# Taking a row maximum ahead of the PSUM ring reads of its tick, and holding back GpSimd's bias copies, in a software-pipelined attention kernel

## What is computed

```python
x = x + _L0_conv_ref(_gn(x), Wq, Wk, Wv, Wo, rel_pos_bias, particle_rel_pos_bias)   # softmax attention, 8 heads, additive bias
t = _to_tokens(x)
t = t + _L1_attn_ref(_ln_t(t), Wq, Wk, Wv, W1, b1, w2, b2)                          # additive attention
t = t + _L1_ffn_ref(_ln_t(t), gate_w, w1, b1, w2, b2)                               # 8 experts, top 2
```

```python
A = jnp.einsum('bse,he->bsh', q, W1[:, :e]) + b1
B = jnp.einsum('bse,he->bsh', k, W1[:, e:])
hidden = jnp.tanh(A[:, :, None, :] + B[:, None, :, :])
logits = jnp.einsum('bijh,h->bij', hidden, w2) + b2[0]
attn = jax.nn.softmax(logits, axis=-1)
return jnp.einsum('bij,bjd->bid', attn, v)
```

## Time and profile before

| | |
|---|---|
| median of 3 executions | 2275.16 us |
| the three | 2275.16, 2265.41, 2275.72 us |
| the profiled execution: its time | 2264.8 us |
| its span, first to last instruction | 2263.0 us |
| mean granted TensorE clock | 0.979 |
| busy share PE, ACT, DVE, POOL | 91%, 74%, 69%, 68% |
| L1510, L1512 and L952 | 96 of each |

### The profile page before, as it was taken

One profiled execution on the slowest core, in us unless ns is written; L12 is line 12 of the kernel. 1 busy time (PEld: TensorE's weight loads), 2 busy tenths in 40 slices (PEclk: granted clock), 3 DMA queues, 4 the chain that ended last, 5 costly groups with the idle time before them and its releaser, 6 DMA issues.

```text
span 2263.0 us, 54452 instructions
## 1 busy us (share of the span) xinstructions
PE 2056.6 (91%) x19545; PEld 1203.6 (53%) x19545; DVE 1550.5 (69%) x4167; ACT 1682.2 (74%) x1966; POOL 1535.5 (68%) x1907
## 2 busy tenths in 40 slices
PE   4889999999999999999999999999999978799996
PEld 2555555555555555455555555555545443367775
DVE  7786777777777787878787878787867554324343
ACT  4449888888887878888888888888879998524332
POOL 5117667677676767676767676767677876347777
PEclk8799999999999999999999999999999999999998
DMA  4746322222322232223223232323221000035553
GB/s 108 111 86 145 93 46 69 48 63 47 72 50 72 51 71 51 71 52 69 53 63 59 61 60 60 58 59 54 58 44 26 13 5 6 24 57 87 85 88 34
DMA packets 157429, 137.41 MB, mean 61 GB/s; under 512 B 24666, under 2 KB 149815, under 8 KB 157105
## 3 DMA queue, kind: packets, MB, share of 16 engines
q1 hardware_dynamic: 119376, 109.87, 23.8%
q0 software_dynamic: 23824, 16.85, 5.4%
q10 hardware_dynamic: 13968, 7.30, 1.3%
HBM read 82.68 MB, written 54.52 MB: 61 GB/s over the span
## 4 chain that ended last, share of the span: by engine, by line
PE 29%; DVE 18%; issue 16%; POOL 14%; POOLq 10%; DVEq 5%; ACT 5%; DMA 1%; another core or an unknown queue 0%; SPq 0%; ACTq 0%
POOL hidden L847 10%; PE logits L1052 8%; POOLq L846 7%; POOL out_dram L601 4%; DVE max_halves L1324 3%; PE av_bank L1038 3%; PE ring L1130 3%; PE ring L1144 2%; ACT hidden L969 2%; PE scores L1022 2%; PE scores L1025 2%; ACT hidden L976 2%; PE ring L1152 2%; PE ring L1121 1%; DVE logit_bias L1510 1%
## 5 line engine op out<-in xcount | busy, mean ns | idle before, releaser
L847 POOL TENSOR_SCALAR hidden<-b_rep,a_cols 128x768 f32<-128x768 f32 x1120 | 1026.8, 921 | 415.3 <-issue 232.2
L969 ACT ACTIVATE hidden<-hidden 128x2304 f32<-128x2304 f32 (+1 forms) x384 | 796.1, 2073 | 52.9 <-POOL hidden L847 52.8
L1052 PE MATMUL logits<-hidden,w_shifted 128*32 128x384 f32 x6144 | 580.6, 494 | 58.2 <-ACT hidden L976 31.1
L1324 DVE TENSOR_REDUCE max_halves<-ring 128x4 f32<-128x512 f32 (+1 forms) x704 | 451.0, 659 | 156.8 <-PE ring L1130 150.9
L945 ACT ACTIVATE probs<-scores 128x512 f32<-128x512 f32 (+1 forms) x768 | 391.5, 547 | 202.5 <-PE scores L1025 195.9
L976 ACT ACTIVATE hidden<-b_rep,a_cols 128x768 f32<-128x768 f32 x416 | 385.0, 933 | 0.0
L1052 PEld LDWEIGHTS logits<-hidden,w_shifted 128*32 128x32 f32 x6144 | 163.4, 109 | 290.8 <-issue 227.4
L1130 PE MATMUL ring<-k_max,q_max 112*128 112x128 bf16 x2688 | 270.3, 223 | 17.2 <-DVE max_halves L1324 12.8
L1022 PE MATMUL scores<-bias_q,onehot_k 112*128 112x512 bf16 (+1 forms) x768 | 273.9, 357 | 4.1 <-DMA q_parts<-max_parts 1.8
L1025 PE MATMUL scores<-q_parts,k_parts 98*128 98x256 bf16 (+1 forms) x1536 | 275.0, 260 | 0.0
L1130 PEld LDWEIGHTS ring<-k_max,q_max 112*128 112x128 bf16 x2688 | 180.9, 99 | 157.9 <-issue 66.3
(11 more groups left out here) (274 smaller groups left out, 2611.7 us busy)
## 6 DMA issues: line engine op xcount, KB each, us to landing
qk_parts<-qk_parts_sb SPq DMA_DIRECT2D x16, 1152.0 KB, 4.3
q_parts<-qk_parts SPq DMA_DIRECT2D x192, 96.0 KB, 3.2
k_parts<-qk_parts SPq DMA_DIRECT2D x192, 96.0 KB, 4.4
q_max<-qk_parts SPq DMA_DIRECT2D x96, 96.0 KB
k_max<-qk_parts SPq DMA_DIRECT2D x96, 96.0 KB
expert_rows<-clear_row ACTq DMA_DIRECT2D x9, 792.0 KB, 5.2
x_in<-in_x_dram SPq DMA_DIRECT2D x96, 64.0 KB
x<-in_x_dram SPq DMA_DIRECT2D x96, 64.0 KB
```

The lines of the kernel that those rows point to most:

```text
L847: last = g.tensor_scalar(hidden[:, q % SLOTS, o, :], b_rep[:, side], 1.0, a_cols[:, side, a_col(q, o):a_col(q, o) + 1], ALU.mult, ALU.add)
L969: s.activation(hidden[:, t % SLOTS, 0:n_, :], hidden[:, t % SLOTS, 0:n_, :], ACT.Tanh)
L1052: last = mm(logits[32 * g:32 * g + 32, half, 0:HALF], w2_shifted[:, k, :], hidden[:, q % SLOTS, g, HALF * half:HALF * half + HALF], start= ...
L1324: v.tensor_reduce(max_halves[:, h % 4:h % 4 + n_, BLOCK_PAIRS.index((qb, kb))], bank[:, 0:n_ * P].rearrange("p (h k) -> p h k", h=n_), AX. ...
```

## The change

DVE's block of maximum and bias moves from the end of slot 1, after the reads, to slot 0, ahead of the reads of its tick. GpSimd waits for `parts_ready` to reach 4 before its first bias copy. No instruction is added or taken out besides that wait.

```diff
@@ GpSimd, prepare()
                 g.memset(flag[:, 0:1], 0.0).then_inc(bias_made, 1)
+                pool.wait_ge(parts_ready, 4)
                 for h in range(H):
                     last = g.tensor_copy(bias_q[0:64, h, :].rearrange("p (b n t) -> p b n t", n=16, t=8),
@@ VectorE, body(ps)
                     for slot in range(PARTS):
-                        for use in parts[slot]:
-                            if ps.has(use[0]):
-                                read(ps, use)
-                        if t % 4 == 0 and slot == 1 and ps.has(stage) and blk >= 0:
+                        if t % 4 == 0 and slot == 0 and ps.has(stage) and blk >= 0:
                             c = ps.batch(stage)
                             dve.wait_ge(logits_added, c * 24 + 4 * (blk + 1))
                             if positive(count := c * 6 + blk):
@@
                             dve.drain()
                             v.tensor_scalar(logit_bias[:, 1:2], logit_bias[:, 0:1], b2_col[:], b2_col[:], ALU.subtract,
                                             ALU.add).then_inc(max1_ready, 1)
+                        for use in parts[slot]:
+                            if ps.has(use[0]):
+                                read(ps, use)
```

## The result

The changed kernel is slower: its median is 2291.53 us (2287.85 to 2296.0, five executions) where the kernel before has 2269.34 (2261.03 to 2275.72) in the same series. The ratio is 1.0103, its 95% interval 1.0076 to 1.0129: 1.0% slower, 22 us. The forecast was no change, 2270 us, and its range ended at 2283. The profiled execution's span is 2293.5 us (before 2263.0), the mean granted clock 0.973 (before 0.979).

A forecast was written before the change was run, and what follows sets the result against it. No single engine was taken to set the pace; the chain changes hands between PE, DVE and GpSimd. Terms -1.8 - 1.1 = -2.9 us, from the two levels' mean 2270.3, gave 2267.4, leaned to 2270 us; range 2253 to 2283.

The forecast's parts named there:

- Ticks 4 and 0: Earlier maximum gives PE 0.91 us at tick 4 and at most 0.38 at tick 0, up to 1.29 us by tick 7.
- not under 35: Sign to look for: ScalarE's waits ahead of its exponential L952 fall from 70.8 to under 35 us.
- the first rival: GpSimd doesn't decide: every full pass keeps its 1.29 us, 17.9 us or 0.8% faster; chance 0.15.
- Tick 7: "nothing ahead of them has moved": In nine passes GpSimd's sums decide when the tanh ends; nothing ahead of those sums moved, so the gain is zero.
- The term of 0.9 us in four passes: At tick 7, passes 1, 5, 6 and 7 have about 1 us of slack and keep 0.9 us each.
- Tick 8: 0.45 us lost, net 1.8 us: Later read of ring use 8.0 costs PE 0.45 us in four passes, leaving 4 x (0.9 - 0.45) = 1.8 us gained.
- Tick 12: Read of 12.1 comes 1.33 us later, within 1.66 us of slack: no effect.
- the rival that VectorE starves: Late ring reads at tick 12 leave DVE an empty ring: +14.4 us, 0.6% slower; chance 0.11.
- Tick 16: "Nothing is queued behind it that PE needs sooner": Cast L1408 goes behind the maximum; DVE is 0.56 us late, at most 1.47, under 1.64 us of idle time: no cost.
- my own price if the cover were gone: At tick 16, without idle time to absorb DVE's lateness, the cost would be 13 x 0.56 = 7.3 us.
- Tick 20: Only the order of DVE's maximum and the two cuts of the transpose changes: no effect.
- GpSimd's copies: In the head, held-back bias copies shorten DVE's second long subtraction from 1684 to 558 ns, 1.13 us gained.

The follow-up runs named there:

- max_0_4_fetch_32: Kernel before with the maximum ahead at ticks 0 and 4, the bias wait and eight dummy matmuls (32 instructions) in PE's head: 2272.89 us, ratio 1.0016.
- after_fetch_32: The whole changed kernel with 32 more instructions in front of PE's program: 2283.29 us, ratio 1.0059 to the kernel before.
- max_8_12_20: Kernel before with the maximum ahead at ticks 8, 12 and 20 only, no bias wait: 2267.52 us, ratio 0.9988.
- max_8_to_20_hold: Kernel before with the maximum ahead at ticks 8, 12, 16 and 20, the bias wait, and GpSimd's tick 21 sums held: 2261.98 us, ratio 0.9968.
- the hold: GpSimd's sums of tick 21 wait until DVE has made the first three normalized heads; added to the whole changed kernel: 2274.13 us, ratio 1.0026 to before.
- max_not_16: Changed kernel with tick 16 alone undone (maximum ahead at ticks 0, 4, 8, 12, 20, with the bias wait): 2280.93 us, ratio 1.0063 to before.
- bias_alone: Kernel before with only GpSimd's wait ahead of its bias copies, every maximum in its old place: 2267.88 us, ratio 0.9993.
- max_16: Kernel before with the maximum ahead at tick 16 alone, no bias wait: 2281.92 us, ratio 1.0064.
- max_16_hold: Kernel before with the maximum ahead at tick 16 alone, and GpSimd's sums of tick 21 held until three heads are made: 2260.49 us, ratio 0.9971.
- fetch_48: Kernel before with twelve dummy matmuls (48 instructions) in PE's head: 2298.38 us, ratio 1.0129.
- fetch_32: Kernel before with eight dummy matmuls (32 instructions) in PE's head: 2267.42 us, ratio 1.0007.
- hold_alone: Kernel before with only GpSimd's sums of tick 21 held until the first three heads are made: 2267.34 us, ratio 0.9995.
- max_0_4: Kernel before with the maximum ahead at ticks 0 and 4 only, with the bias wait: 2284.17 us, ratio 1.0075.

## Why the prediction was wrong, point by point

- **Ticks 4 and 0.** Half right. PE gains 0.70 us a pass by product 1 (8.4 us in twelve passes), more than the 0.38 forecast; at tick 4 ScalarE's 0.91 us of idle time is gone and PE's 0.46 us wait is down to 0.19 in pass 4. The further 0.91 us come in full in five of twelve passes only (5 and 9 to 12, where PE is 1.67 to 1.73 us early at product 5); in the sum products 4 and 5 have 4.8 us less than before. In pass 4 the tanh ahead of the exponential already waits 2.37 us for GpSimd, so GpSimd decides sooner than at tick 7. ScalarE's waits ahead of the exponential fell from 70.8 to 53.9 us, not under 35. Nor do 0.70 and 0.46 us in each of 13 passes, 15 us, make up most of PE's 56.3 us of waiting for ScalarE, as the first rival has it.
- **Tick 7: "nothing ahead of them has moved".** The first step that failed. That GpSimd decides and the gain is given back was right (max_0_4_fetch_32: 8.4 us won, 10.6 given back). But I let the relation between engines out: GpSimd is held by the burst, PE isn't, so PE's instruction fetch comes sooner against GpSimd's last indirect DMA. The collision costs 8 us in the changed kernel (after_fetch_32), 11 us with ticks 0 and 4 alone. No term and no rival had it. The changed kernel has two passes without the third stop, 9 and 10, and there PE is still 2.34 and 1.22 us early at product 7. In the ten others it is 0.1 us early to 2.5 us late. The term of 0.9 us in four passes can't be told from this.
- **Tick 8: 0.45 us lost, net 1.8 us.** Not seen in the changed kernel: in passes 1 to 12 the intervals behind products 7 and 8 differ by 0.2 us in all. PE isn't early there, since GpSimd has taken that back. Where ticks 0 and 4 are as before, the one behind product 7 is longer by 2.3 us (max_8_12_20) and 2.5 us (max_8_to_20_hold), 0.2 us a pass.
- **Tick 12, and the rival that VectorE starves.** Nothing, as forecast. The slower side came, by another mechanism.
- **Tick 16: "Nothing is queued behind it that PE needs sooner".** The step that cost most: 14.6 us with this swap alone, 10.6 when it alone is undone, 17 by the hold, of 22 us. I looked for the next idle time of DVE, 1.64 us, and not at what stands between: the copy `headsT_raw`, which PE waits for, and the subtractions, which SyncE's store waits for. Even my own price if the cover were gone, 7.3 us, was too small, since the delay of 0.7 us is only a part of the cost. The later store lets GpSimd's DMA land in 2.1 us instead of 4.5, GpSimd's stop of 1.9 us goes, and its sums fall on DVE's heads, which makes three instructions of 0.86 us last 2.06. An engine that became sooner did the harm, and I had asked only which become later. The rule of the Trainium skill ("SBUF — State Buffer", "Who interferes with whom"), that of the two the one waits for the other's whole instruction, was the right one. In pass 2 the three heads take 0.35, 0.94 and 0.94 us, the last two about as long as one of GpSimd's sums (0.91). I priced it at the cast (0.99 us instead of 0.56, so it holds there too) and not at the next place where both meet.
- **Tick 20.** Right in itself: max_not_16 has its order changed and no longer waits.
- **GpSimd's copies.** Not seen. In the changed kernel the second subtraction takes 1104 ns, not 558: with the copies gone it lies beside GpSimd's addition L825, as the first does. PE's first scores start 0.25 us sooner there (75.03 instead of 75.28). In bias_alone the two last subtractions do take 558 ns each, but the two ahead of them 1102, and the first scores start at 75.66. Its time is that of before, so the term of 1.1 us was worth nothing that can be measured.

The lower clock is part of the price. No run takes it apart, but the traces do. The step from product 19 to product 20 holds PE's wait for the heads, and in some passes one stretch at the lower of the two levels (1.2 instead of 2.4 GHz), which begins 4 to 8 us behind product 19. Means of this step in us, passes 1 to 12 (number of passes):

| kernel | full clock | with a stretch of 3.4 us | with one of 6.8 us |
|---|---|---|---|
| before | 8.53 (9) | 10.07 (3) | none |
| changed | 8.89 (7) | 10.53 (3) | 11.90 (2) |
| max_16 | 8.99 (9) | 10.44 (2) | 12.39 (1) |
| max_16_hold | 7.90 (12) | none | none |
| after_fetch_32 | 8.74 (3) | 10.62 (6) | 11.87 (3) |
| fetch_48 | 8.65 (1) | 11.47 (3) | 12.52 (8) |

At full clock the changed kernel loses 0.36 us a pass here, 4.3 us in twelve; the other 6.3 of its 10.6 us are the stretches (10.9 us in five passes, before 4.6 in three). In fetch_48 eleven of twelve passes have one. At the prices of the changed kernel's rows these come to some 24 of its 36 us at this step, an estimate. What makes the clock fall isn't shown: it falls at this place in none of the traces in which PE doesn't wait for the heads, but neither in fetch_32, hold_alone or max_not_16, in which it does.

## What to carry to other kernels

Where an instruction is delayed, look not at the next idle time of its engine but at every instruction between it and that idle time, and ask of each who waits for it, and whom it will now run beside. Ask also whose stop goes away by the delay: an engine that comes sooner can do more harm than the one that comes late. A gain of one engine shifts it against all that are paced by something else; what met nobody before, an instruction fetch or a port, can meet them in every pass. Where a small edit costs more than its own work, lengthen one engine's program by a few idle instructions in the head: if the time jumps, the code is being timed by where its fetches fall.

## What the hardware showed that I had not expected

A fetch of PE's program is one packet of 16 KB, and takes a DMA engine 0.9 to 1.8 us in the kept traces. An indirect DMA whose packets come then lands late: the one of tick 5 takes 2.0 to 2.3 us from issue to its last packet where no fetch is in its way (before, passes 1 to 12), and 2.8 to 3.8 us where one is (all 13 passes of max_0_4), and GpSimd goes on 0.7 to 1.4 us after that last packet. The Trainium skill, "DMA: Bandwidth & Descriptors", section "Queues, rings and completion order", says that a DMA engine turns from one queue to the next only between whole packets; the packet that starts at 656.97 us, at the end of the fetch, agrees. Whether a packet of the profile is a packet in the page's sense, no run here shows. Since a pass here is 2304 PE instructions, nine times 256, the phase is the same in all passes, and twelve dummy matmuls cost 30 us. That it is the same DMA engine is inferred from the times; the trace doesn't name it. The kernel before can meet the fetch too: in bias_alone, with every maximum in its old place, the third stop stands in passes 4 and 8 (1.45 and 1.60 us). And 0.63 us between GpSimd's DMA and a store of 1152 KB behind it decide over 2.4 us of landing time.
